# Order of work inside a channel's slot, exchanged X by DMA for most channels, and the third input in the fill

## What is computed

```python
def _get_kernel(log_dt, C, log_A_real, A_imag, length):
    Cc = C[..., 0] + 1j * C[..., 1]
    dt = jnp.exp(log_dt)
    A = -jnp.exp(log_A_real) + 1j * A_imag
    dtA = A * dt[:, None]
    P = dtA[:, :, None] * jnp.arange(length, dtype=jnp.float32)
    Cs = Cc * (jnp.exp(dtA) - 1.0) / A
    return 2.0 * jnp.einsum('hn,hnl->hl', Cs, jnp.exp(P)).real
...
mask = (jnp.arange(Lq) < length[:, None])
u_m = u * mask[:, None, :]
y = causal_conv(u_m, kernel)[..., :Lq] + u_m * D[:, None]   # by FFT of length 2 * Lq
x = x + y * mask[:, None, :]
```

## Time and profile before

| | |
|---|---|
| median of 3 runs | 862.51 us |
| profiled execution | 864.69 us |
| its span | 862.8 us |
| TensorE matmul busy | 821.8 us, 95% of the span |
| VectorE busy | 743.1 us, 86% |
| ScalarE busy | 674.4 us, 78% |
| GpSimd busy | 603.6 us, 70% |
| DMA queue of the program | 65.9% of 16 engines |

### The profile page before, as it was taken

The page is one execution under the profiler, slowest core; times in us unless marked ns, Lnnn a source line. Parts: engine busy times, 40 slices in busy tenths (PEclk is TensorE's granted clock), DMA queues, the critical chain, the costliest instruction groups (busy, mean ns, idle before and its releaser), DMA issues.

```text
span 862.8 us, 23096 instructions
## 1 busy us (share of the span) xinstructions
PE 821.8 (95%) x6299; PEld 787.6 (91%) x6299; DVE 743.1 (86%) x2041; ACT 674.4 (78%) x1722; POOL 603.6 (70%) x847
## 2 busy tenths in 40 slices
PE   0779999999999999999999999999999999999997
PEld 0668999999999999999999999999999999999996
DVE  7857898888888888888888888888888888888886
ACT  4667887878788887878787878888787878787874
POOL 5965767667676767677776767676767777776763
PEclk9989999999999999999999999999999999999999
DMA  4133677777676776767676767677676767676764
GB/s 106 34 84 94 185 198 185 193 178 191 188 194 188 191 191 185 193 185 193 184 190 187 195 185 193 188 192 190 186 195 181 197 181 197 181 193 186 197 186 135
DMA packets 161394, 152.73 MB, mean 177 GB/s; under 512 B 13656, under 2 KB 161240, under 8 KB 161240
## 3 DMA queue, kind: packets, MB, share of 16 engines
q1 hardware_dynamic: 161064, 152.15, 65.9%
q10 hardware_dynamic: 304, 0.26, 0.1%
HBM read 84.02 MB, written 67.30 MB: 175 GB/s over the span
## 4 chain that ended last, share of the span: by engine, by line
PE 88%; ACT 3%; DMA 3%; DVE 3%; SPq 1%; issue 1%; POOL 0%; DVEq 0%; ACTq 0%; POOLq 0%
PE y L1110 15%; PE y L1111 13%; PE y L1112 13%; PE y L1158 12%; PE xt_even L1095 6%; PE xt_odd L1095 6%; PE v L1110 6%; PE v L1112 6%; PE v L1111 6%; DMA xall<-in_x_dram 3%; PE y L1105 2%; PE y L1106 2%; SPq L369 1%; ACT B L585 0%; DVE zlo L1021 0%
## 5 line engine op out<-in xcount | busy, mean ns | idle before, releaser
L585 ACT ACTIVATE room<-v 64x192 f32<-64x192 f32 (+1 forms) x768 | 236.4, 308 | 27.5 <-PE v L1112 2.4
L968 DVE SCALAR_TENSOR_TENSOR mid<-room,RV,v 128x192 f32<-128x192 f32 (+2 forms) x512 | 185.1, 361 | 73.8 <-ACT room L585 55.9
L557 POOL TENSOR_TENSOR uol<-uod,uoh 128x448 fp32r<-128x448 f32 x85 | 98.4, 1158 | 139.9 <-issue 139.9
L968 DVE SCALAR_TENSOR_TENSOR v<-v,RV,mid 128x192 f32<-128x192 f32 (+2 forms) x512 | 177.7, 370 | 16.5
L1110 PE MATMUL y<-thi,uhi 128*128 128x256 f32 x511 | 186.4, 365 | 0.0
L957 DVE COPY_PREDICATED xall<-mask,y 128x512 f32<-128x512 int32 x254 | 178.2, 752 | 1.4 <-issue 1.3
L538 POOL TENSOR_TENSOR room<-W,B 128x256 f32 (+1 forms) x254 | 161.8, 637 | 23.5 <-POOL room L547 11.1
L1110 PE MATMUL y<-fhi,zhi 128*128 128x256 f32 x511 | 153.7, 301 | 3.2 <-DVE zlo L1021 3.2
L1112 PE MATMUL y<-fhi,zlo 128*128 128x256 f32 x511 | 144.2, 282 | 0.0
L1111 PE MATMUL y<-tlo,uhi 128*128 128x256 f32 x511 | 144.1, 282 | 0.0
L1111 PE MATMUL y<-flo,zhi 128*128 128x256 f32 x511 | 144.1, 282 | 0.0
(11 more groups left out here) (223 smaller groups left out, 1987.1 us busy)
## 6 DMA issues: line engine op xcount, KB each, us to landing
xall<-in_x_dram SPq DMA_DIRECT2D x256, 256.0 KB, 4.3
out_dram<-xall SPq DMA_DIRECT2D x254, 256.0 KB, 3.4
traw<-krows SPq DMA_DIRECT2D x128, 128.0 KB, 3.0
NXY<-B SPq DMA_DIRECT2D x2, 512.0 KB, 6.3
krows<-ksb SPq DMA_DIRECT2D x8, 1.0 KB, 2.1
krows<-ksb SPq DMA_DIRECT2D x8, 4.0 KB, 3.8
krows<-ksb SPq DMA_DIRECT2D x8, 11.0 KB, 3.8
out_dram<-xall SPq DMA_DIRECT2D x1, 128.0 KB, 2.4
```

The source lines that it names most:

```text
L557: pool.tensor_tensor(uol[j % 2][:], uod[j % 3][:, 0:EVERY], uoh[j % 2][:].bitcast(F32), ALU.subtract).then_inc(s_uol, 1)
L585: return act.activation(dst, src, ACT.Copy)
L968: return dve.scalar_tensor_tensor(out=out, in0=src, scalar=RV[:, k:k + 1, h], in1=other, op0=ALU.mult, op1=ALU.add)
```

## The change

On ScalarE `z_high` of here stands ahead of `x_odd` of two, and `x_odd` behind `turn_pairs` of one. On VectorE `x_low` of two stands behind `z_low` and `fours_turned`, and `e_low` behind `fours`. The exchanged table X2 is turned by TensorE and copied by ScalarE for the first 8 channels only (EARLY); for channels 8 to 127 SP copies the two halves of W1[:, 0] crosswise into W2 in slot 0 (`swap_x`), and channel 8's second product waits for it. The sign moves from X2 to B2, so the difference of the products becomes a sum (`whole_table`). The last two copies of X1 go to VectorE (BY_VECTOR). The transposes of channel 2's x, and `x_odd_high` and `odd_low` of channel 1, move from slot 0 into the fill. On GpSimd the two mask comparisons move behind the first table product, and VectorE waits for them in slot 1. The diff, shortened by lines that only follow from these (layout of W2, names, semaphores):

```diff
@@ -36,12 +36,13 @@
          ("B1", 12), ("B2", 12), ("Y1", 12), ("Y1", 8), ("B1", 8), ("B2", 8),
-         ("X1", 12), ("X2", 12), ("X1", 8), ("X2", 8), ("B1", 0), ("B1", 4), ("B2", 0), ("B2", 4),
-         ("X1", 0), ("X1", 4), ("X2", 0), ("X2", 4), ("Y1", 0), ("Y1", 4), ("S", 0)]
-T_K = len(STEPS)
+         ("X1", 12), ("X1", 8), ("X2", 8), ("B1", 0), ("B1", 4), ("B2", 0), ("B2", 4),
+         ("X1", 0), ("X1", 4), ("X2", 0), ("Y1", 0), ("Y1", 4), ("S", 0)]
+EARLY = 8
 K_GROUPS = [range(0, 1), range(1, 5), range(5, 9), range(9, 13), range(13, 16)]
-SIGNED = ("X2", "Y1")
-ROWS = ("B1", "B2", "X1", "Y1")
+SIGN = {("R", 1): 1, "Y1": 0, "B2": 1, "S": 2}
+BY_VECTOR = [STEPS.index(("X1", 0)), STEPS.index(("X1", 4))]
...
@@ -276,6 +278,10 @@
             return t[:, 0:NC * B].rearrange("p (c b) -> p c b", b=B)
+        def first(g, j):
+            return isinstance(g, int) and chan(g, j) == 0
...
@@ -322,13 +328,14 @@
                 return RV[:, 6, :]
-            if name in ROWS:
-                return {"B1": B1[:], "B2": B2[:], "X1": W1[:, 0], "Y1": W1[:, 1]}[name][:, :, i:i + 4]
-            return W2[:, i:i + 4, :]
+            if name == "X2":
+                return W2[:, 0:EARLY, i:i + SQ // 2]
+            return {"B1": B1[:], "B2": B2[:], "X1": W1[:, 0], "Y1": W1[:, 1]}[name][:, :, i:i + 4]
         def sign(t):
-            return {("R", 1): sgn[:, 1:2], ("S", 0): sgn[:, 2:3]}.get(STEPS[t], sgn[:, 0:1] if STEPS[t][0] in SIGNED else None)
+            column = SIGN.get(STEPS[t], SIGN.get(STEPS[t][0]))
+            return None if column is None else sgn[:, column:column + 1]
@@ -369,6 +376,11 @@
                                  ).then_inc(s_out[j], 16)
+            def swap_x(half):
+                to, by = (slice(a * N, a * N + N) for a in (half, 1 - half))
+                sp.dma_start(W2[to, EARLY:, :], W1[by, 0, EARLY:, :]).then_inc(s_swap, 16)
...
@@ -424,6 +436,9 @@
                     load_t(*on(g, j, 2))
+                if first(g, j):
+                    for half in range(2):
+                        swap_x(half)
@@ -512,10 +527,6 @@
                   [q1, q3, mag_flat, wide], 3, 0, 4).then_inc(s_ypool, 1)
-            for n in range(2):
-                part = mask[:, n * 512:(n + 1) * 512]
-                pool.tensor_scalar(part, part, flen[:, 0:1], None, ALU.is_lt).then_inc(s_mask, 1)
@@ -531,13 +542,15 @@
                 h = chan(g, j)
-                w = (W1[:, 0, h, :], W2[:, :, h])[which].unsqueeze(2).broadcast_to([P, SQ, SQ])
+                w = (W1[:, 0, h, :], W2[:, h, :])[which].unsqueeze(2).broadcast_to([P, SQ, SQ])
...
                     pool.wait_ge(s_pf, h - 1)
+                if which == 1 and isinstance(g, int) and h == EARLY:
+                    pool.wait_ge(s_swap, 16 * 2)
                 pool.tensor_tensor((tw1, tw2)[which], w, b, ALU.mult).then_inc(s_gpa, 1)
-            def difference(g, j):
+            def whole_table(g, j):
...
@@ -564,19 +577,23 @@
                 f_low(*here)
-                if has1:
+                if has1 and not first(g, j):
...
                 if has2:
-                    difference(*two)
-            tables_placed(pool, ("X2", 4))
+                    whole_table(*two)
+            odd_low(0, 0)
+            tables_placed(pool, ("X2", 0))
             product(0, 1, 1)
-            difference(0, 1)
-            odd_low(0, 0)
+            whole_table(0, 1)
+            for n in range(2):
+                part = mask[:, n * 512:(n + 1) * 512]
+                pool.tensor_scalar(part, part, flen[:, 0:1], None, ALU.is_lt).then_inc(s_mask, 1)
+            odd_low(0, 1)
@@ -636,6 +653,8 @@
                 for t in range(STEPS.index(first), STEPS.index(last) + 1):
+                    if t in BY_VECTOR:
+                        continue
@@ -646,7 +665,7 @@
             def double_x(i):
-                copy(NXY[:, i, 0, 2, :], NXY[:, i, 0, 0, :]).then_inc(s_xdup, 1)
+                copy(NXY[0:EARLY, i, 0, 2, :], NXY[0:EARLY, i, 0, 0, :]).then_inc(s_xdup, 1)
@@ -663,22 +682,20 @@
             take(("Y1", 8), ("B2", 8))
-            act.wait_ge(s_nx, 1)
-            double_x(slice(12, 16))
-            take(("X1", 12), ("X2", 12))
+            take(("X1", 12), ("X1", 12))
             act.wait_ge(s_nx, 2)
-            double_x(slice(8, 12))
+            double_x(slice(SQ // 2, SQ))
...
             double_b(slice(0, SQ // 2))
-            take(("B1", 0), ("B2", 4))
             double_x(slice(0, SQ // 2))
-            take(("X1", 0), ("X2", 4))
+            take(("B1", 0), ("B2", 4))
             act.wait_ge(s_ny, 3)
-            tables_placed(act, ("X2", 4))
+            tables_placed(act, ("B2", 4))
             copy(b0[:, 1], B2[:, 0, :]).then_inc(s_b0, 1)
+            take(("X2", 0), ("X2", 0))
@@ -747,16 +764,17 @@
                     x_high(*two)
-                    x_odd(*two)
...
                 if has2:
+                    x_odd(*two)
...
             x_odd(0, 1)
+            x_odd_high(0, 1)
...
@@ -1026,6 +1044,8 @@
                 has0, has1, has2, hasb = exists(g, j, 0), exists(g, j, 1), exists(g, j, 2), exists(g, j, -1)
+                if isinstance(g, int) and h == 1:
+                    dve.wait_ge(s_mask, 2)
@@ -1037,15 +1057,16 @@
                     pairs(*one)
-                if has2:
-                    x_low(*two)
...
                 if has2:
+                    x_low(*two)
+                if has1:
+                    fours(*one)
+                if has2:
                 if has1:
-                    fours(*one)
@@ -1054,8 +1075,11 @@
                     add_d(slice(5, SQ))
+            for t in BY_VECTOR:
+                filled(dve, t)
+                dve.tensor_copy(place(t), four(t)).then_inc(s_free[t % BANKS], 1)
             dve.wait_ge(s_b0, 1)
-            tables_placed(dve, ("X2", 4))
+            tables_placed(dve, ("X2", 0))
@@ -1067,7 +1091,6 @@
             sixth(0, 0)
-            dve.wait_ge(s_mask, 2)
@@ -1178,7 +1201,7 @@
                     odd_sums(*one)
-                if has2:
+                if has2 and not first(g, j):
...
@@ -1215,11 +1238,16 @@
                         pe.wait_ge(s_free[t % BANKS], t // BANKS)
-                    for r in range({"R": 3, "S": 1}.get(STEPS[t][0], 4)):
-                        dst = pro[t % BANKS][:, r * P:(r + 1) * P]
-                        if STEPS[t][0] in ROWS:
+                    name = STEPS[t][0]
+                    n = EARLY if name == "X2" else P
+                    for r in range({"R": 3, "S": 1, "X2": SQ // 2}.get(name, 4)):
+                        if name in ("R", "S"):
+                            dst = pro[t % BANKS][:, r * P:(r + 1) * P]
+                        elif name == "X2":
+                            dst = pro[t % BANKS][:, r:EARLY * SQ // 2:SQ // 2]
+                        else:
                             dst = pro[t % BANKS][:, r:512:4]
-                        mm = pe.transpose(dst, source(t, r).rearrange("p c n -> p (c n)"), ident[:])
+                        mm = pe.transpose(dst, source(t, r)[0:n].rearrange("p c n -> p (c n)"), ident[0:n, 0:n])
@@ -1265,15 +1293,15 @@
                 turn(("X1", i), ("X1", i))
-                pe.wait_ge(s_xdup, k)
-                turn(("X2", i), ("X2", i))
+            pe.wait_ge(s_xdup, 1)
+            turn(("X2", 8), ("X2", 8))
...
             turn(("X1", 0), ("X1", 4))
-            pe.wait_ge(s_xdup, 3)
-            turn(("X2", 0), ("X2", 4))
+            pe.wait_ge(s_xdup, 2)
+            turn(("X2", 0), ("X2", 0))
@@ -1289,6 +1317,8 @@
             turn_e(0, 1)
+            turn_x(0, 2, 0)
+            turn_x(0, 2, 1)
```

More of the change, by code:

```diff
@@ L86, in s4d_kernel @@
         W1 = sb("W1", [P, 2, H, SQ])
-        W2 = sb("W2", [P, SQ, H])
+        W2 = sb("W2", [P, H, SQ])
         B1 = sb("B1", [P, H, SQ])
@@ L202, in s4d_kernel @@
         s_gpa = sem("s_gpa")
+        s_swap = sem("s_swap")
         s_yini = sem("s_yini")
@@ L313, in four @@
                 return pro[t % BANKS][:, 0:H]
-            if name in ROWS:
-                return pro[t % BANKS][:].rearrange("p (h i) -> p h i", i=4)
-            return pro[t % BANKS][:].rearrange("p (i h) -> p i h", h=H)
+            if name == "X2":
+                return pro[t % BANKS][:, 0:EARLY * SQ // 2].rearrange("p (h i) -> p h i", h=EARLY)
+            return pro[t % BANKS][:].rearrange("p (h i) -> p h i", i=4)
         def place(t):
@@ L398, in _ @@
                 load_t(0, j)
-            tables_placed(sp, ("X2", 4))
+            tables_placed(sp, ("X2", 0))
             sp.dma_start(bsel[0:N], B1[0:N]).then_inc(s_bsel, 16)
@@ L547, in difference @@
                 pool.tensor_tensor(pf[j % 2], tw1.rearrange("p b c -> p (b c)"),
-                                   tw2.rearrange("p b c -> p (b c)"), ALU.subtract).then_inc(s_pf, 1)
+                                   tw2.rearrange("p b c -> p (b c)"), ALU.add).then_inc(s_pf, 1)
             def odd_low(g, j):
@@ L933, in first_table @@
             def first_table():
```

(6 more changed lines are left out.)

## The result

The changed kernel takes **896.04 us** (median of 4 runs, 895.94 to 896.94). The kernel before took 862.56 us beside it (4 runs, 862.41 to 863.89). The ratio is 1.0387, with a 95% interval of 1.0369 to 1.0405: slower by 3.9%. The forecast was 886 with a range of 866 to 894. The direction was right, and the time lies 2 us outside the range. The profiled execution took 895.97 us, its span is 894.0 us against 862.8, so 31.2 us are to be found.

A forecast was written before the change was run, and what follows sets the result against it. The chain from the last sum through the states, zhi and zlo, not TensorE's work, was taken to set the 6.23 us loop. Terms 27.0 + 2.8 - 0.4 - 5.0 - 1.0 = +23.4 led to 886 us, range 866 to 894.

The forecast's parts named there:

- uol's margin of 0.22: Loop slot, GpSimd's uol to TensorE's odd sums: the odd sums could start at 411.86 but start at 412.08.
- the ring: Loop slot: odd sums, zhi, uoh, uol, next odd sums; claimed to set the new period, 6.49 us against 6.48 taken.
- the loop's +27.0: 18 passes of 6 slots: uoh later, uol past its margin, 0.25 us for each of 108 slots; bounds +18 and +31.
- Straight slots: Channels outside the loop: uoh 0.34 later against 0.11 left at uol, 0.23 in some 12 slots, +2.8 us (bounds 1 and 4).
- k_copy: Four slots with k_copy ahead of the x copies: z_high wins 0.5, uol takes back about 0.4; -0.4 us in all.
- late loads: TensorE's four waits for x loads between 110 and 835 us: longer slots give loads time, -1.0 us (bounds 0 and -1.7).
- the -5.0: Fill: tables placed differently and third input early, so the sums of channel 2 start earlier; -5.0 us (bounds -2.4 and -7).
- It costs nothing of its own: VectorE's new order: elo about one x_low later may hold the even sums 0.1 us, but the odd sums wait longer for uol.
- Rival (1): Only the fill changes: ScalarE goes from uhi to zhi at once, uoh does not move; faster, 857 us; chance 0.11.
- Rival (2): Loop: the wait at the state products goes too, zhi 0.17 earlier, -16 us, with the fill 841; chance 0.05.

The follow-up runs named there:

- the kernel with SP's new order: Changed kernel with VectorE's odds ahead of pairs_turned, and on SP the store of h - 1 ahead of load_t of h + 2: 843.55 us, ratio 0.9775.
- the kernel with `odds` first: Changed kernel with one more edit, on VectorE odds ahead of pairs_turned: 846.16 us, ratio 0.9792.
- the kernels with both moves: VectorE's odds ahead of pairs_turned and ScalarE's z_high ahead of x_odd: on the kernel before 851.09 us; on the changed kernel 846.16, with SP's store ahead of load_t 843.55.

## Why the prediction was right, and where it was off

**The bound.** Right. ScalarE's order alone makes the slowdown (1.0425 alone, 0.9993 without it). The argument, that zhi was held by the states and not by x_odd, that the gain is nothing, and that the 0.5 us then comes out of uol's margin of 0.22, is what the rows show: uoh 2.00 behind zhi, ScalarE idle 0.41, uol late in every slot.

**The step that failed** is the term "odd sums 0.78 us" in the ring "odd sums 0.78, last sum to zhi 1.72, zhi to the end of uoh 2.55, then 0.13, 1.16, 0.15: 6.49". The other terms came out within 0.01 each. The odd sums took 0.85: they start behind a wait now, and then the second product starts 0.28 behind the first, not 0.21. I took the 0.78 from a slot in which they ran on without waiting. 0.07 x 108 = 7.6 us, and the loop's +27.0 became +34.6; the upper bound of the term, 31, allowed only for a longer step on ScalarE. The price stood in the earlier trace rows, where the product behind its wait at 52.92 has 0.44, and the same product at 63.10 has 0.37. The 0.29 for 0.12 in the earlier trace rows is no such price: before, the second state product started 0.19 behind the first, and in the kernel with SP's new order, where nothing is waited for there, 0.20 (306.49 to 306.69).

```profile
410.16 0.28 PE L1111 MATMUL y<-flo,zhi 128*128 128x256 f32 x1
```

**The median.** The sum was short by 7.8 us of span, and a further 2.2 us came from carrying it over. The profiled execution of before was 2.2 above its median, and I took the same off the forecast. After, profile and median agree within 0.1. Which of its executions is profiled matters here: those that keep the clock in the fill take 3 us less (below), so a gain taken from the profile's half clock is not all a gain of the median, and taking the 2.2 off as well counts part of it twice. Neither error alone leaves the range: 886 + 7.8 is 893.8, just under 894, and with the 2.2 it is 896.0.

**Straight slots, k_copy, late loads.** +3.9 for +2.8 (6.33 a slot, forecast 6.31, and a later end), -0.2 for -0.4, -2.0 for -1.0. The last is outside its bound: four slots of before were 0.49, 0.38, 0.44 and 0.87 longer than their neighbours, 2.2 in all, where the earlier trace rows lists 1.7 of waiting. Each wait cost about 0.1 more than is listed. Whether that is a restart too, these transposes do not show.

**The fill.** Right in size, in part by luck. The sums of channel 1 start 1.64 earlier (forecast 1.75), the state-free products at 53.03 (53.3), the clock holds, the sums of channel 2 start at 57.97 (57 to 58), and nothing waits for the swap. But the -5.0 was a middle between a clock that holds, -5.8, and one that does not. It held, and the term came to -5.1, because the slot behind 53.03 took 4.94 where the working had about 4.0 at 2.4 GHz. That 4.0 left out the 0.62 that TensorE waits there for zlo. What I did not see either is how much of the gain is the clock that some executions of before keep anyway, and that only 1.4 us of span is left of it once ScalarE's order is back.

**VectorE.** "It costs nothing of its own" holds beside ScalarE's new order (896.58 without it). With ScalarE's old order the loop is 2.7 us longer by the traces; about half of that, the slot with the restart, is VectorE's order, and the rest is not explained.

**FIFO.** The Trainium skill ("PSUM — Partial Sum Buffer", Engine vs sequencer instructions) has the queues of ScalarE, VectorE and GpSimd as strict FIFO. The traces agree: 0.41 us idle ahead of zhi while x_odd's input is long there. Rival (1), the fill's gain alone, needed the opposite. Rival (2), the wait at the states gone as well, is what the kernel with `odds` first does: it needed the earlier states that I said nothing in the diff gives.

**Open.** In the kernels with both moves one slot of each loop pass still takes 0.2 to 0.4 longer than 6.06. Where the swap and VectorE's new order are in, it is the wait for uol (0.27 to 0.28 between the first odd sums, in that slot alone). On the kernel before, where the slot takes 6.45, the odd sums run on at 0.21, and the cause is not known.

## What to carry to other kernels

Write each loop-carried ring with the row of every part, and where a ring is about to become the bound, price its restarts from rows of the same product: the 128x448 sums cost 0.07 more behind a wait, the 128x256 state products showed nothing of the kind. Moving an instruction that waits ahead of one that is ready pays only if what it waits for is made ready first; the two edits together gave 12 us where the one cost 38 and the other gave 2. Before an edit, write down every margin that it spends (uol 0.22, elo 1.04, the store's landing), because the next ring is often only tenths away.

## What was unexpected of the hardware

- The first 128x448 product behind a wait is followed by the next after 0.28 to 0.29 us, in a run after 0.20 to 0.21, at the full clock. It is so behind uol in all loop slots (but one slot of one kernel) of the four kernels that have ScalarE's new order and `odds` in its old place, and behind elo in all 108 of the one with x_odd between z_high and turn_pairs. In the kernel before it is so in none.
- The half clock in the fill does not come in every execution of one kernel. Of 56 executions of before on four chips, the 18 with a mean granted clock of 0.999 or 1.000 took 860.8 us on average, and the 38 with 0.992 to 0.996 took 863.8. Its profile, with 6.83 us of half clock from 53.67 on, is one of the second kind.
- In the kernel whose load waits for the store issued one slot before, that store's landing is 4.27 of a ring of 7.04; the others that were read along its loop landed in 3.9 to 4.5 us, one in 5.44. In the kernel before and in the one with the store ahead of load_t, whose loads come one channel later, no x load waits for a store.
